# Attention scores and their masks issued in four column tiles of 32 keys instead of one of 128

## The chip, the cores and the metric

The kernel runs on one core of a Trainium2 chip. The metric is the device time of one launch in microseconds (us), as a median of several runs. The engines named here are TensorE (PE: matmuls; PEld: the weight loads that go with them), VectorE (DVE), ScalarE (ACT), GpSimd (POOL) and SyncE (SP), which issues the DMAs.

## What is computed

Two attention layers over a graph, for 8 batches of 1024 nodes with 128 features. The first has 8 heads of 16 features, the second one head with additive scores. Cut to what matters:

```python
def first(x, adj):                       # 8 heads of 16
    q, k, v = heads(x @ Wq), heads(x @ Wk), heads(x @ Wv)
    scores = einsum('bhqd,bhkd->bhqk', q, k) / sqrt(16)
    scores = where(adj[:, None] > 0, scores, -1e9)
    return merge(softmax(scores) @ v) @ Wo + bo

def second(x, adj):
    h = x @ W.T
    e = (h @ a1)[:, :, None] + (h @ a2)[:, None, :]
    e = where(e >= 0, e, 0.2 * e)
    return softmax(where(adj > 0, e, -9e15), axis=2) @ h

x = layernorm(x + first(x, adj))
x = layernorm(x + second(x, adj))
```

The change touches the product of q and k and the masking of the scores in the first layer.

## The kernel before

Each engine runs a list of instructions that is written out in full, for 8 batches with 64 positions each. Position u of batch b holds one **unit**: the scores of one head against 128 keys, for all 1024 queries. Four heads share a tile of keys, so units 4n to 4n+3 are the four heads of key tile n (n from 0 to 15: two groups of heads, eight tiles of keys).

What stands at a position on TensorE, in this order:

- `unit(b, u)`, lines 402 to 421. Two matmuls (L415, halves of 512 queries each) put the scores, keys on the partitions, into one of three PSUM slots. The stationary operand is `kst`, 97 rows by 128 keys in bf16; the moving one is `qst`, 97 rows by 512 queries. In 27 of the 64 units, those with an "m" in `MASKED_BY`, two more matmuls (L420) add the mask to the same PSUM, with the identity `same` as the stationary operand. In the other units VectorE multiplies by the mask afterwards (L755).
- `context(b, n)`, lines 423 to 443, at each position with a remainder of 3 by 4, some positions later than its units: the weights of four heads times v. It is already issued in column tiles: head i writes 17 partitions of `acc` from partition 32 i on. In the trace it is 16 matmul records (two for each fp32 matmul of the program), in four rounds of four.
- **Jobs** from the table `PE_AT`: projections q, k, v0 and v1 (L485, L499, L505), the column sums cc (L492), the transposes ctx0, ctx1, ctxT and x1T (L512, L518, L526), wo (L522), h0 and h1 (L532, and L535 with a stationary operand of one column), fi (L540), and the eight sums of the second layer, out0 to out7 (L474, L475). In a batch in the middle of the program jobs stand at the positions 1, 4 to 8, 13, 15, 17, 18, 26, 27, 28, 32, 43, 58 and 63. They are fp32 with 128 stationary columns, but for cc (bf16, 32 columns) and L535.

The language gives each matmul a tile shape by the number of its stationary columns: 128 rows by 128 columns of the array for more than 64, 128 rows by 32 columns for 32 and fewer. Below these are called **wide** and **narrow**. Units and nearly all jobs are wide; contexts, cc and L535 are narrow.

ScalarE takes each unit's slot through the exponential (L584) into `weights`, in the order of the units, with jobs of its own between them; among these are the exponentials of the second layer (exp0 to exp7, L602), at the positions 43 to 61. A slot becomes free for the unit three uses later when ScalarE is done with it (`free_for`, semaphore `exp_done`). TensorE waits for the eight exponentials of the second layer before out1 at position 63, and before the other out jobs at the positions after it.

Of the kernel before, what the change touches and what calls it, by code (L numbers as in the profile page):

```python
# [99 lines left out]
def build_fast(nc, sems, needed, x, xT, adjT, Wq, Wk, Wv, Wo, bo, W, a, out):  # L100
# [5 lines left out]
    T = N // 128  # L106
    HALF = N // 2
# [8 lines left out]
    VW = 32  # L116
# [10 lines left out]
    with ExitStack() as ctx:  # L127
        def sb(name, shape, dt):
            return ctx.enter_context(nc.sbuf_tensor(name, shape, dt))

        def sem(name):
            return sems.enter_context(nc.semaphore(name))
# [8 lines left out]
        same = sb("same", [128, 128], BF16)  # L141
# [23 lines left out]
        masks = [sb(f"mask{i}", [128, T, N], BF16) for i in range(2)]  # L165
        qst = sb("qst", [SROWS, H, N], BF16)
        kst = sb("kst", [SROWS, H, N], BF16)
# [75 lines left out]
        masks_made = sem("masks_made")  # L243
# [23 lines left out]
        def slot_of(name, me, u=0):  # L267
            return slots[slot[name, me, u]]

        def free_for(name, me, u=0):  # L270

            was = holder[name, me, u]
            if was is None:
                return exp_done, 0
            return released(*was)
# [123 lines left out]
        def _(pe):  # L399
            kw = dict(start=True, stop=True)  # L400

            def unit(b, u):
                n, i = divmod(u, HG)
                g, t = divmod(n, T)
                h = g * HG + i
                ps = slot_of("unit", b, u)
                if b == 0 and u == 0:
                    pe.wait_ge(consts_made, 2)
                if u % (UNITS // NG) == 0:
                    pe.wait_ge(stack_in[g], (b + 1) * 16 * STACK_DMAS)  # L410
                pe.wait_ge(*free_for("unit", b, u))
                by_pe = MASKED_BY[u] == "m"
                for c in range(2):
                    cols = slice(c * HALF, (c + 1) * HALF)
                    mm = pe.matmul(ps[:, cols], kst[:, h, t * 128:(t + 1) * 128], qst[:, h, cols], start=True, stop=not by_pe)  # L415
                if by_pe:
                    pe.wait_ge(masks_made, b * T + t + 1)
                    for c in range(2):
                        cols = slice(c * HALF, (c + 1) * HALF)
                        mm = pe.matmul(ps[:, cols], same[:], masks[b % 2][:, t, cols], start=False, stop=True)  # L420
                mm.then_inc(full["unit"], 1)

            def context(b, n):
# [132 lines left out]
            for b in range(-1, B + 2):  # L556
                for pos in range(UNITS):
                    if 0 <= b < B:
                        unit(b, pos)
                    if at := context_at(b, pos, B):  # L560
                        context(*at)
                    for name, me in jobs_at(PE_AT, b, pos, B):
                        job(name, me)
                        if me == 0 and name == "k":
                            fold_second_layer()
                    if b == -1 and pos == UNITS - 1:
                        pe.wait_ge(usq_made, 1)
                        pe.matmul(acc[:, 384:386], ones[:], usq[:], **kw).then_inc(unorm_mm, 1)
# [1100 lines left out]
```

## Time and profile before

| | us |
|---|---|
| median of 3 runs | 925.04 (923.72 to 925.59) |
| the profiled execution's own time | 921.75 |
| its span, first to last instruction | 920.0 |
| TensorE busy (matmuls) | 844.0, 5485 records |
| weight loads busy | 406.5, 5485 records |
| VectorE busy | 686.2 |
| ScalarE busy | 635.3 |

Matmuls are pipelined: a record lasts longer than the time to the start of the next one, and a busy TensorE is not one at its peak. So the text goes by the starts. A line of a timeline gives the start of a group of instructions and the time from there to the group's end; the difference between the starts of two lines is what the first one costs TensorE. In a line such as "128\*17 128x512 f32 x16" the first pair is rows and columns of the stationary operand, the second is the moving operand, and the last is the number of records.

### The profile page before, as it was taken

How to read it: one execution, taken by the hardware profiler on the slowest of the kernel's cores; microseconds unless marked ns; L12 is line 12 of the kernel's file. 1: busy time of each engine (PE TensorE's matmuls, PEld its weight loads, DVE VectorE, ACT ScalarE, POOL GpSimd, SP SyncE). 2: the span in 40 equal slices, each digit the busy share in tenths (PEclk: the TensorE clock that was granted, in tenths of full speed). 3: DMA queues.
4: the chain of work that ended last, by engine and by line, in shares of the span. 5: the costliest groups of instructions: out<-in, count | busy, mean ns of one | idle time of the engine just before them, and what ended most of it. 6: DMA issues, size and time to landing. Idle time of an engine off the chain costs nothing.

```text
span 920.0 us, 14889 instructions
## 1 busy us (share of the span) xinstructions
PE 844.0 (92%) x5485; PEld 406.5 (44%) x5485; DVE 686.2 (75%) x1157; ACT 635.3 (69%) x702; POOL 65.5 (7%) x47
## 2 busy tenths in 40 slices
PE   5499999999999999999999999999999999998683
PEld 2132334327533474336543374334743366324573
DVE  5276797895878868896878868787687966796463
ACT  2378886995579846896579945898378965796050
POOL 3000010001010100101010010101010010101000
PEclk9599999999999999999999999999999999999877
DMA  4877258603556227544377136363275234401000
GB/s 158 158 135 154 38 163 161 111 7 109 110 120 105 81 92 94 138 58 126 82 149 100 39 102 118 115 94 90 83 136 110 44 105 96 54 2 35 1 24 26
DMA packets 50926, 85.56 MB, mean 93 GB/s; under 512 B 5969, under 2 KB 23122, under 8 KB 50834
## 3 DMA queue, kind: packets, MB, share of 16 engines
q1 hardware_dynamic: 50850, 84.57, 44.2%
q8 instruction: 45, 0.74, 0.4%
q14 instruction: 31, 0.25, 0.1%
HBM read 67.63 MB, written 16.91 MB: 92 GB/s over the span
## 4 chain that ended last, share of the span: by engine, by line
PE 69%; ACT 16%; issue 8%; DVE 5%; DMA 0%; POOL 0%; POOLq 0%; SPq 0%; ACTq 0%; DVEq 0%
PE acc L441 18%; PE slot L415 17%; PE slot L474 11%; ACT weights L584 11%; PE slot L420 8%; ACT atts L602 4%; PE slot L485 3%; PE slot L522 2%; PE slot L532 2%; DVE weights L755 1%; PE slot L475 1%; PE slot L458 1%; PE slot L512 1%; DVE atts L769 1%; PE slot L526 1%
## 5 line engine op out<-in xcount | busy, mean ns | idle before, releaser
L584 ACT ACTIVATE weights<-slot 128x1024 f32<-128x1024 f32 x512 | 496.1, 1048 | 169.4 <-PE slot L415 94.1
L755 DVE SCALAR_TENSOR_TENSOR weights<-mask,weights 128x1024 f32<-128x1024 bf16 x296 | 359.3, 1239 | 65.4 <-ACT weights L584 64.2
L415 PE MATMUL slot<-qst,kst 97*128 97x512 bf16 x1024 | 287.3, 383 | 26.9 <-issue 14.6
L441 PE MATMUL acc<-weights,vst 128*17 128x512 f32 x2048 | 244.6, 595 | 7.1 <-DVE weights L755 6.5
L415 PEld LDWEIGHTS slot<-qst,kst 97*128 97x128 bf16 x1024 | 84.7, 98 | 213.2 <-ACT weights L584 87.2
L420 PE MATMUL slot<-mask,same 128*128 128x512 bf16 x432 | 129.8, 381 | 0.0
L474 PEld LDWEIGHTS slot<-hst,atts 128*128 128x128 f32 x896 | 105.8, 191 | 19.4 <-issue 9.2
L474 PE MATMUL slot<-hst,atts 128*128 128x129 f32 x896 | 110.7, 276 | 3.0 <-ACT atts L602 3.0
L441 PEld LDWEIGHTS acc<-weights,vst 128*17 128x17 f32 x2048 | 47.9, 96 | 141.1 <-issue 127.5
L769 DVE SCALAR_TENSOR_TENSOR atts<-turn,hst,mask 128x1024 f32<-128x1024 f32 x64 | 83.5, 1310 | 6.8 <-ACT hst L652 6.8
L845 DVE RECIPROCAL rout<-slot 128x1 f32<-128x1 f32 x62 | 10.4, 167 | 91.0 <-PE slot L475 82.4
L602 ACT ACTIVATE atts<-atts,expbias 128x1024 f32<-128x1024 f32 x64 | 75.4, 1224 | 1.7 <-DVE atts L769 1.1
L420 PEld LDWEIGHTS slot<-mask,same 128*128 128x128 bf16 x432 | 42.4, 98 | 52.1 <-issue 1.1
L708 POOL TENSOR_TENSOR rstd<-vareps,exponent 128x4 f32<-128x4 f32 (+1 forms) x24 | 33.9, 1413 | 393.6 <-DVE vareps L825 393.6
L713 POOL TENSOR_TENSOR x_sb<-x_sb,bo_all 128x1024 f32<-128x1024 f32 x8 | 22.5, 2808 | 437.9 <-DMA x_sb<-in_x 437.9
L780 DVE TENSOR_SCALAR mask<-raw 128x1024 bf16<-128x1024 int32 x64 | 48.1, 753 | 6.4 <-DMA raw<-in_adjT 6.4
L618 ACT ACTIVATE atts<-slot 128x1024 bf16<-128x1024 f32 x16 | 16.4, 1023 | 23.6 <-PE slot L485 23.6
L830 DVE TENSOR_SCALAR x<-y,meanvar,rstd 128x128 f32<-128x128 f32 x64 | 17.1, 343 | 14.5 <-POOL rstd L708 14.5
L793 DVE TENSOR_TENSOR atts<-slot,atts 128x1024 f32<-128x1024 f32 x16 | 19.6, 1224 | 11.2 <-issue 11.0
L641 ACT ACTIVATE turn<-slot 128x1024 f32<-128x1024 f32 x8 | 8.2, 1023 | 26.0 <-PE slot L518 26.0
L846 DVE SCALAR_TENSOR_TENSOR x<-slot,rout,x 128x128 f32<-128x128 f32 x62 | 21.8, 351 | 2.2
L864 DVE TENSOR_REDUCE widest<-slot 64x1 f32<-64x1024 f32 x8 | 9.7, 1216 | 17.2 <-issue 10.0
(117 smaller groups left out, 580.3 us busy)
## 6 DMA issues: line engine op xcount, KB each, us to landing
raw<-in_adjT SPq DMA_DIRECT2D x64, 512.0 KB, 4.1
parts_scratch<-atts SPq DMA_DIRECT2D x48, 256.0 KB, 2.5
qst<-parts_scratch SPq DMA_DIRECT2D x96, 128.0 KB
kst<-parts_scratch SPq DMA_DIRECT2D x96, 128.0 KB
xT_sb<-in_xT SPq DMA_DIRECT2D x8, 512.0 KB, 4.6
x_sb<-in_x SPq DMA_DIRECT2D x8, 512.0 KB, 5.4
out<-x SPq DMA_DIRECT2D x16, 256.0 KB, 2.3
qst<-shift_scratch SPq DMA_DIRECT2D x16, 8.0 KB
```

The source lines that it names most:

```text
L415: mm = pe.matmul(ps[:, cols], kst[:, h, t * 128:(t + 1) * 128], qst[:, h, cols], start=True, stop=not by_pe)
L420: mm = pe.matmul(ps[:, cols], same[:], masks[b % 2][:, t, cols], start=False, stop=True)
L441: mm = pe.matmul(acc[VW * i:VW * i + HD + 1, cols], vst[b % 2][:, t, g * HG + i], weights[:, HG * buffer(b, n) + i, cols], start=(t == 0), ...
L474: pe.matmul(to, att_of(j, k), hst[:, j, 0:D + 1], start=(j == 0), stop=False)
L485: mm = pe.matmul(ps[:, cols], (wq if name == "q" else wk)[:], xT_sb[:, cols], **kw)
L584: act.activation(to, ps[:], ACT.Exp, scale=SCALE).then_inc(exp_done, 1)
L602: act.activation(atts[:, :, j, :], atts[:, :, j, :], ACT.Exp, bias=expbias[:, j:j + 1]).then_inc(atts_made, 1)
L708: pool.tensor_tensor(rstd[i][:, tt], vareps[i][:, tt], exponent[:, tt], ALU.pow).then_inc(rstd_made[k], 1)
L713: pool.tensor_tensor(x_sb[:], x_sb[:], bo_all[:].unsqueeze(1).to_broadcast([128, T, D]), ALU.add).then_inc(xb_made, 1)
L755: dve.scalar_tensor_tensor(out=to, in0=masks[b % 2][:, n % T], scalar=0.0, in1=at, op0=ALU.is_equal, op1=ALU.mult).then_inc(masked, 1)
L769: dve.scalar_tensor_tensor(out=atts[:, :, j, :], in0=fi_all[:].rearrange("p (q n) -> p q n", q=4), scalar=hst[:, j, D + 1:D + 2], in1=mask ...
L780: dve.tensor_scalar(masks[b % 2][:, t], raw[m][:], 0, -BIG, ALU.is_le, ALU.mult).then_inc(masks_made, 1)
```

## The change

In `unit` each matmul is split into four by keys: tile i takes 32 columns of `kst` and writes the partitions 32 i to 32 i + 31 of the slot. The mask matmuls are split in the same way by columns of `same`. The order is by halves of the queries, and within one by tiles. The wait for the mask (`masks_made`) stands ahead of the scores instead of between scores and mask. Everything else, the tables included, stays.

```diff
                 pe.wait_ge(*free_for("unit", b, u))
                 by_pe = MASKED_BY[u] == "m"
+                if by_pe:
+                    pe.wait_ge(masks_made, b * T + t + 1)
                 for c in range(2):
                     cols = slice(c * HALF, (c + 1) * HALF)
-                    mm = pe.matmul(ps[:, cols], kst[:, h, t * 128:(t + 1) * 128], qst[:, h, cols], start=True, stop=not by_pe)
-                if by_pe:
-                    pe.wait_ge(masks_made, b * T + t + 1)
-                    for c in range(2):
-                        cols = slice(c * HALF, (c + 1) * HALF)
-                        mm = pe.matmul(ps[:, cols], same[:], masks[b % 2][:, t, cols], start=False, stop=True)
+                    for i in range(4):
+                        rows = slice(VW * i, VW * (i + 1))
+                        keys = slice(t * 128 + VW * i, t * 128 + VW * (i + 1))
+                        mm = pe.matmul(ps[rows, cols], kst[:, h, keys], qst[:, h, cols], start=True, stop=not by_pe)
+                for c in range(2 if by_pe else 0):
+                    cols = slice(c * HALF, (c + 1) * HALF)
+                    for i in range(4):
+                        rows = slice(VW * i, VW * (i + 1))
+                        mm = pe.matmul(ps[rows, cols], same[:, rows], masks[b % 2][:, t, cols], start=False, stop=True)
                 mm.then_inc(full["unit"], 1)
```

The program's TensorE list around the positions 15 to 17 of a middle batch, before. A row names the line, the operands (out <- in), the columns of the stationary operand by those of the moving one, and the semaphores that it waits for. L441 is the context, L518 the job ctxT, L522 the job wo.

```order
L420 MATMUL slot<-mask,same 128x512
L441 MATMUL acc<-weights,vst 17x512 [waits masked,exp_done]
L441 MATMUL acc<-weights,vst 17x512 x7
L518 MATMUL slot<-ident,turn 128x128 [waits ctx0_taken,q_taken]
L518 MATMUL slot<-ident,turn 128x128 x3
L518 MATMUL slot<-ident,turn 128x128 [waits ctx1_taken]
L518 MATMUL slot<-ident,turn 128x128 x3
L415 MATMUL slot<-qst,kst 128x512 [waits exp_done]
L415 MATMUL slot<-qst,kst 128x512
L420 MATMUL slot<-mask,same 128x512 [waits masks_made]
L420 MATMUL slot<-mask,same 128x512
```

The same place after, where the lines are five higher (L415 is L420, L420 is L425, L441 is L446, L518 is L523, L522 is L527):

```order
L425 MATMUL slot<-mask,same 32x512 x8
L446 MATMUL acc<-weights,vst 17x512 [waits masked,exp_done]
L446 MATMUL acc<-weights,vst 17x512 x7
L523 MATMUL slot<-ident,turn 128x128 [waits ctx0_taken,q_taken]
L523 MATMUL slot<-ident,turn 128x128 x3
L523 MATMUL slot<-ident,turn 128x128 [waits ctx1_taken]
L523 MATMUL slot<-ident,turn 128x128 x3
L420 MATMUL slot<-qst,kst 32x512 [waits masks_made,exp_done]
L420 MATMUL slot<-qst,kst 32x512 x7
L425 MATMUL slot<-mask,same 32x512 x8
L420 MATMUL slot<-qst,kst 32x512 [waits exp_done]
L420 MATMUL slot<-qst,kst 32x512 x7
L527 MATMUL slot<-wo,turn 128x128 [waits ctxT_taken]
```

No instruction changed places. The shape changes from wide to narrow and back have: before, one stood ahead of the context (128 to 17 columns) and one behind it; after, none stands ahead of the context, one ahead of the transposes, one behind them, and one more ahead of wo, which had none before. Over the whole program, counted in the two lists, 274 changes of shape become 224: batch by batch 29 become 9 in batch 0, 35 become 23 in batch 1, 34 become 32 in each of the batches 2 to 6, and 38 become 30 in batch 7 with what follows it; 2 stand ahead of the first unit in both.

## Rows read from the trace of the kernel before

**Rows 1.** Busy time of each engine in stretches of the span.

```profile
core 0: us, PE busy (x) PEld busy (x) DVE busy (x) ACT busy (x) POOL busy (x), PEclk, DMA share, GB/s
43.00:117.60 74.60, 72.64 (x443) 24.07 (x442) 53.44 (x55) 61.72 (x67) 0.00 (x0) 1.00 0.61 121
...
314.30:390.62 76.32, 75.84 (x509) 40.81 (x510) 57.31 (x114) 49.19 (x54) 6.93 (x4) 1.00 0.53 119
390.62:420.70 30.08, 27.95 (x177) 9.20 (x175) 27.30 (x28) 29.88 (x34) 0.00 (x0) 1.00 0.38 51
```

**Rows 2.** Timeline of TensorE near the end of the second stretch.

```profile
413.62 1.91 PE L441 MATMUL acc<-weights,vst 128*17 128x512 f32 x16 [0.72 <-DVE weights L755]
...
420.70 2.02 PE L474 MATMUL slot<-hst,atts 128*128 128x129 f32 x16 [0.55 <-ACT atts L602]
```

**Rows 3.** Timeline of ScalarE at the same place.

```profile
416.54 1.94 ACT L584 ACTIVATE weights<-slot 128x1024 f32<-128x1024 f32 x2 [0.20 <-PE slot L420]
```

**Rows 4.** Timeline of TensorE: two units, a context, the next unit.

```profile
362.65 1.03 PE L415 MATMUL slot<-qst,kst 97*128 97x512 bf16 x4
363.52 0.60 PE L420 MATMUL slot<-mask,same 128*128 128x512 bf16 x2
364.05 1.91 PE L441 MATMUL acc<-weights,vst 128*17 128x512 f32 x16
365.89 0.60 PE L415 MATMUL slot<-qst,kst 97*128 97x512 bf16 x2
```

**Rows 5.** Timeline of TensorE: context, cc, and the wait behind fi.

```profile
370.33 1.91 PE L441 MATMUL acc<-weights,vst 128*17 128x512 f32 x16
372.06 0.60 PE L492 MATMUL slot<-atts,headsum 128*32 128x512 bf16 x4
372.59 0.61 PE L415 MATMUL slot<-qst,kst 97*128 97x512 bf16 x2
...
375.40 1.51 PE L415 MATMUL slot<-qst,kst 97*128 97x512 bf16 x6 [0.48 <-ACT negshift L624]
```

**Rows 6.** Timeline of TensorE: an out job behind another, and one behind a context.

```profile
431.82 1.95 PE L474 MATMUL slot<-hst,atts 128*128 128x129 f32 x16
433.61 0.39 PE L475 MATMUL slot<-hsum,ones 128*128 128x129 f32 x2
...
440.39 2.05 PE L474 MATMUL slot<-hst,atts 128*128 128x129 f32 x16
442.28 0.39 PE L475 MATMUL slot<-hsum,ones 128*128 128x129 f32 x2
```

**Rows 7.** Timeline of TensorE: transposes behind a context and wo; transposes behind a unit.

```profile
351.37 1.09 PE L518 MATMUL slot<-ident,turn 128*128 128x128 f32 x8
352.30 0.60 PE L415 MATMUL slot<-qst,kst 97*128 97x512 bf16 x2
...
353.16 0.59 PE L415 MATMUL slot<-qst,kst 97*128 97x512 bf16 x2
353.66 2.02 PE L522 MATMUL slot<-wo,turn 128*128 128x128 f32 x16
355.52 0.60 PE L415 MATMUL slot<-qst,kst 97*128 97x512 bf16 x2
...
368.50 1.03 PE L526 MATMUL slot<-ident,x 128*128 128x128 f32 x8
369.37 0.60 PE L415 MATMUL slot<-qst,kst 97*128 97x512 bf16 x2
```

**Rows 8.** Timeline of TensorE: h0 and h1, then their one-column matmul.

```profile
379.13 1.95 PE L532 MATMUL slot<-wh,turn 128*128 128x130 f32 x16
381.01 0.38 PE L535 MATMUL slot<-wh,x1sum 128*1 128x128 f32 x2
381.32 1.04 PE L415 MATMUL slot<-qst,kst 97*128 97x512 bf16 x4
```

**Rows 9.** Groups by line: the context's matmuls.

```profile
L441 PE MATMUL acc<-weights,vst 128*17 128x512 f32 x2048 | 244.6, 595 | 7.1 <-DVE weights L755 6.5 <-ACT weights L584 0.6
```

## The prediction

> **What bounds the kernel now.** I read the busy time by stretch first, then the timeline of TensorE inside each stretch, by the starts of its groups. A batch in the middle of the program lasts 106.40 us and has two parts. In the first, 76.32 us from the job out1 to the exponential of unit 40, TensorE is busy for 75.84 us and ScalarE for 49.19; in the second, 30.08 us, ScalarE is busy for 29.88 and TensorE for 27.95 [rows 1]. So TensorE sets the first part. In the second, where the exponentials of the second layer stand, ScalarE does, and TensorE waits for others: 0.72 us ahead of a context and 0.55 us ahead of out1 [rows 2]. Work taken off TensorE pays in the first part alone. Batch 0 has no second part: TensorE is busy for 72.64 of 74.60 us, ScalarE for 61.72 [rows 1].
>
> **What a unit costs.** Two pairs of wide matmuls take 363.52 − 362.65 = 0.87 us, so 0.435 a pair [rows 4]. For a pair in narrow tiles the nearest row is the context: with nothing to switch behind it, its four rounds of four tiles take 372.06 − 370.33 = 1.73 us [rows 5], 0.4325 a round. A round of fp32 there lasts as long as two of bf16, and four tiles run in it at once. The last of the four starts about 1.91 − 3 × 0.4325 − 0.595 = 0.02 us behind the first [rows 4, 9], and this lag is not paid again in each round, or the four would not fit in 1.73. So a narrow pair should cost 0.432: 0.003 less than a wide one. Bounds: no gain, and a loss of 0.04 (the lag paid in both rounds; third rival). The first part of a batch has 41 units and 20 masks, 61 pairs: −0.18 us; batch 0, with all its 91 pairs, −0.27.
>
> **What a change of shape costs.** Into a context: 364.05 − 363.52 is 0.53, 0.095 over the pair. Out of a context to a unit: 365.89 − 364.05 is 1.84, 0.11 over 1.73 [rows 4, 5]. From a wide job to a narrow matmul: 381.01 − 379.13 is 1.88 behind h1, against 433.61 − 431.82 = 1.79 for as many records without a switch, 0.09 [rows 6, 8]. Into an fp32 job more is lost than the 0.11: the out job behind a context takes 442.28 − 440.39 = 1.89 against 1.79, 0.10 more [rows 6], and eight transposes take 352.30 − 351.37 = 0.93 against 369.37 − 368.50 = 0.87, 0.06 more [rows 7]. I read these as the first weights, which cannot be loaded while the array still drains. So a context among wide units costs 0.095 + 0.11 = 0.205. After the change, a wide job among narrow units costs 0.11 + 0.10 + 0.095 = 0.305, or 0.265 where it begins with transposes. The job's price is the context's turned round, plus the load.
>
> The Trainium skill says in "TensorEngine Tiling (Array Packing)", section Tiling Modes, that changing the mode, not just the tile, drains TensorE; it has no figure, and says nothing of a load behind the drain. By that rule alone jobs would cost what contexts did, which is the first rival; the 0.10 of the out job speaks against it.
>
> **The sum for a middle batch (2 to 6), first part.** Removed: ten contexts, at the positions 3 to 39. Ten entries, 10 × 0.095 = 0.95; seven exits to units, 0.77; exits to out6 (position 7) 0.21 and to ctxT (15) 0.17. The exit at 27 leads to cc, which is narrow already, and costs nothing. Also gone: the exit of L535 behind h1 (0.10, bounded by cc's exit, 372.59 − 372.06 less 0.43 [rows 5]). Its entry, 0.09, stays and is counted on both sides. Together 2.29. Added: six jobs that begin with matmuls (positions 1, 4, 5, 7, 13, 18), 1.83; three with transposes (6, 8, 26), 0.795; ctxT 0.265; h0 and h1, 0.21 + 0.09 = 0.30; the exit of out1 into unit 0, 0.095. For wo, of 0.305, some 0.14 is paid today: it waits 353.66 − 353.16 − 0.435 = 0.065 and takes 355.52 − 353.66 = 1.86 against 1.79 [rows 7]; 0.165 is left. Job fi adds nothing: TensorE waits 0.48 us behind it for ScalarE's negshift [rows 5], whose chain begins at cc, and both switches, 0.31, fit into that wait with cc's exit, 0.10, that goes. If this cover were gone, 0.31 us a batch. Together 3.45. Net +1.16, less 0.18 for the pairs.
>
> Second part: ScalarE's row is broken once, for 0.20 us, by a unit that TensorE brings late [rows 3], just behind the context at 413.62. That context's exit goes: −0.11. The other switches of this part lie under ScalarE's work. So a middle batch gains 1.16 − 0.18 − 0.11 = **+0.87 us**, five of them +4.35.
>
> **The other batches.** Batch 0 has 15 contexts and few jobs. Gone: 15 entries 1.425, 13 exits 1.43, one exit to v0 0.21; together 3.065 (the 16th exit-like switch, cc's, lies in the wait for negshift). Added: q, k and v1, 0.915, and v0, 0.305. Net −1.845, with the pairs −2.1. Batch 1 has no out jobs within its first part: removed 2.19 (no 0.10 of load for out6), added ctx0 and ctx1 0.53, q 0.305, ctxT and wo 0.43, k 0.305, x1T 0.265, h 0.30, so 2.135; with −0.18 and −0.11, −0.35. Batch 7 is a middle one without k (−0.305), with fi uncovered (+0.305, no cc) and the exit at 27 gone as well (−0.11): +0.76.
>
> **Total:** 4.35 − 2.1 − 0.35 + 0.76 = +2.7 us. The profiled execution took 921.75 us, 3.3 below the median of the runs shown; the sum is made against it, 924.4, and carried to the median: 925.04 + 2.7 = **927.7 us**.
>
> **What costs nothing.** The mask's wait now stands ahead of the scores. Behind it on TensorE's queue stand the whole unit and all that follows; but TensorE never waited at the mask's matmuls inside a unit (they start 0.435 behind the scores [rows 4]), so the mask is ready before. What could make it late is VectorE, whose masks precede their units by several positions. Each pair has four times the instructions; in the context 16 matmuls and 16 loads pass in 1.73 us, 54 ns each, and a narrow pair needs 16 in 0.432, 27 ns each. No row shows that rate held for long; it is part of the third rival. ScalarE gets each unit at most 0.02 us later, which matters only where it waits on TensorE.
>
> **The rivals.**
>
> First, not slower: entering a job behind a bf16 unit costs no load. The 0.10 was seen behind the context's fp32 rounds alone. Then each middle batch loses 0.97 of the 3.45 and 0.16 of the 2.29, and comes out at +0.06 (five: +0.3), batch 0 at −2.4, batch 1 at −0.85, batch 7 at −0.05: −3.0 in all, **922.0 us**. It decides once an entry costs under about 0.05. Against it: both kinds of fp32 job show the loss. Further down still, if all 50 switches fewer were bare gains of 0.1, −5 and −1.6 for the pairs, 918.5.
>
> Second, neutral: the terms are as I have them but batch 0 and the covers give 1 to 2 us more than I counted, 926. It is the lower half of my forecast, not a mechanism of its own.
>
> Third, much slower: the four tiles' lag of 0.02 us is paid in every round, because a round of bf16 lasts half as long as the context's, or instructions cannot follow at 27 ns. With 91 + 7 × 61 = 518 pairs on the path, 0.04 each is +20.7: **948 us**. At the context's 54 ns an instruction a pair would take 0.86 and the kernel some 220 us more. Against it: cc's four bf16 matmuls, in two tiles, pass in 0.53 with an exit in it, so two rounds take 0.43 [rows 5]; but that is two tiles, not four. The Trainium skill reports in "TensorE: Matmul & The Clock Gate", section Measured speedup vs the span model, a speedup of 2.38 for three column tiles, not 3. An estimate by that page would make a round about a quarter longer and the kernel some 57 us slower; the context's rounds show no such loss.
>
> Fourth, that the tiles do not run side by side at all: excluded by the context, where four tiles take 1.73 us and not four times that.
>
> **How the numbers follow.** Forecast 0.62, with its own range of 925 to 931 (the pairs' gain nil, +1.6; fi's cover gone, +1.9; loads smaller, −2). First rival 0.14, second 0.06, third with its smaller forms 0.18. The range for 8 in 10 is 921 to 940: it takes in half of the first rival, and the third up to some 0.025 us a pair. A measurement of this kernel can tell about 0.2%, 1.85 us: 923.2 and 926.9 are the bounds. Of the forecast a bit over half lies above 926.9, nearly all the rest between; with the rivals: faster 0.13, same 0.34, slower 0.53.
>
> **What would show it.** On TensorE's timeline after: pairs at 0.43; unit to context without the 0.095; context to unit in 1.73; an out job behind a unit in 1.89 instead of 1.79, its exit 0.09 more; h1 to the next unit without a switch. By stretch: a first part of about 77.3 us, a second of 30.0, a middle batch of 107.3, batch 0 two us shorter. Wrong if pairs are above 0.44 (third rival), if entries to jobs cost under 0.16 (first), or if TensorE's waits in the first part grow.

## The result and the profile after

The changed kernel takes **931.03 us** (median of 4 runs, 928.91 to 931.21) against 925.32 us for the kernel before on the same chip (median of 4, 923.72 to 925.95): a ratio of 1.0059, with a 95% interval of 1.004 to 1.0079. It is slower by 5.7 us, where 2.7 was forecast. The profiled executions took 928.91 and 921.75 us, 7.2 apart.

The head of the page of the changed kernel; TensorE has 9853 matmuls and as many weight loads instead of 5485:

```profile
span 927.2 us, 23841 instructions
...
PE 847.1 (91%) x9853; PEld 437.9 (47%) x9853; DVE 687.1 (74%) x1157; ACT 638.1 (69%) x702; POOL 64.9 (7%) x47
```

The stretches that answer to [rows 1], with the same columns: batch 0 from the exponential of unit 4 on, then the two parts of a middle batch.

```profile
43.08:117.50 74.42, 70.66 (x960) 27.99 (x955) 53.18 (x55) 62.25 (x68) 0.00 (x0) 1.00 0.60 121
316.06:393.35 77.29, 76.89 (x882) 43.30 (x882) 58.12 (x114) 49.54 (x55) 6.97 (x4) 1.00 0.50 118
393.35:423.32 29.97, 27.74 (x357) 10.35 (x349) 27.30 (x28) 29.87 (x35) 0.00 (x0) 1.00 0.38 54
```

The first part is 0.97 us longer than before (77.29 against 76.32), the second 0.11 shorter (29.97 against 30.08); both are what was forecast. Batch 0 is not: it was to lose two microseconds. In this table the length of a batch is the time from its first exponential to that of the next batch, in the two profiled executions (the first and the last two rows say where they begin and end; exponentials are taken at their starts):

| stretch | before | after | change | forecast |
|---|---|---|---|---|
| up to the first exponential | 37.75 | 37.96 | +0.21 | 0 |
| batch 0 | 79.87 | 79.54 | −0.33 | −2.1 |
| batch 1 | 93.01 | 94.16 | +1.15 | −0.35 |
| batches 2 to 5, each | 106.39 | 107.25 | +0.86 | +0.87 |
| batch 6 | 106.39 | 107.88 | +1.49 | +0.87 |
| batch 7, to its last exponential | 98.59 | 99.20 | +0.61 | +0.76 |
| from there to the end | 78.86 | 79.45 | +0.59 | 0 |

The prices of the switches come out as forecast. TensorE's timeline after, units, a context, the next unit, as [rows 4]:

```profile
366.00 1.05 PE L420 MATMUL slot<-qst,kst 97*32 97x512 bf16 x16
366.87 0.61 PE L425 MATMUL slot<-mask,same 128*32 128x512 bf16 x8
367.31 1.89 PE L446 MATMUL acc<-weights,vst 128*17 128x512 f32 x16
369.02 0.61 PE L420 MATMUL slot<-qst,kst 97*32 97x512 bf16 x8
```

Two narrow pairs take 0.87 us, as two wide ones did. The context follows a pair after 0.44 us instead of 0.53, and the next unit follows the context after 1.71 instead of 1.84. The same timeline at an out job behind units, which answers to [rows 6], and at wo and x1T, which answer to [rows 7]:

```profile
345.91 1.04 PE L420 MATMUL slot<-qst,kst 97*32 97x512 bf16 x16
346.87 2.05 PE L479 MATMUL slot<-hst,atts 128*128 128x129 f32 x16
348.76 0.39 PE L480 MATMUL slot<-hsum,ones 128*128 128x129 f32 x2
...
356.26 0.60 PE L420 MATMUL slot<-qst,kst 97*32 97x512 bf16 x8
356.80 2.05 PE L527 MATMUL slot<-wo,turn 128*128 128x128 f32 x16
358.78 0.61 PE L420 MATMUL slot<-qst,kst 97*32 97x512 bf16 x8
...
371.19 0.61 PE L425 MATMUL slot<-mask,same 128*32 128x512 bf16 x8
371.73 1.09 PE L531 MATMUL slot<-ident,x 128*128 128x128 f32 x8
372.75 0.61 PE L420 MATMUL slot<-qst,kst 97*32 97x512 bf16 x8
```

The out job takes 348.76 − 346.87 = 1.89 behind a unit, as behind a context before. Job wo starts 0.54 behind its unit's pair and takes 1.98, 0.19 more than a job without switches: 0.105 + 0.19 = 0.295 in all, forecast 0.305. The transposes x1T take 1.02, 0.15 more than among wide units: 0.255 with the entry, forecast 0.265.

**Where the rest went.** In batch 0 and in batch 1 TensorE stops in the middle of a group. Its timeline, first in a unit's mask matmuls, then in a context:

```profile
70.02 0.61 PE L420 MATMUL slot<-qst,kst 97*32 97x512 bf16 x8
70.45 0.38 PE L425 MATMUL slot<-mask,same 128*32 128x512 bf16 x2
72.52 0.61 PE L425 MATMUL slot<-mask,same 128*32 128x512 bf16 x6 [1.68 <-issue]
```

```profile
151.96 0.59 PE L446 MATMUL acc<-weights,vst 128*17 128x512 f32 x1
153.05 1.48 PE L446 MATMUL acc<-weights,vst 128*17 128x512 f32 x12 [0.49 <-issue]
```

From the start of the second tile of a mask's round to that of the third pass 2.06 us, and from the first tile of a context's first round to the second 1.08; in the other masks and contexts of the eight batches it is 0.02 or less, but for 0.19 in the mask that follows the first pause. "issue" means that the profile shows nothing that TensorE waited for; a semaphore cannot be it, since no wait stands inside a group. The two together are 3.1 us of the 4.5 by which the forecast missed the 7.2 of the profiled executions. Both stand at the same remainder: counting TensorE's recorded instructions (matmuls, weight loads, waits) from the first, the pauses come ahead of number 961 and number 3009, 193 + 3 × 256 and 193 + 11 × 256.

The queues of the page, before and then after, with their packets, MB and share, show what has this period:

```profile
q8 instruction: 45, 0.74, 0.4%
```

```profile
q8 instruction: 80, 1.31, 0.6%
```

Queue 8 brings 16 KB a packet (1.31 MB by 80), one for some 256 instructions of TensorE: its program has 11789 instructions before and 20741 after. So a packet is used up in about 920.0 / 45 = 20 us before and 927.2 / 80 = 11.6 after. Read over the eight batches of the changed kernel, the packet of a block starts at about the time at which the block ahead of it begins: for 52 of 74 blocks between 2.4 us before that and 1.6 us after. The others start later, up to 8.4 us after, and the blocks of the two pauses are among the latest three. For the block whose first instruction is number 961 the block ahead begins at 61.8, and this is what the DMA engines did from then to 69.3 us, and from 69.3 to 71.2:

```profile
DMA packets 530, 0.86 MB, mean 114 GB/s; under 512 B 111, under 2 KB 111, under 8 KB 530
## 3 DMA queue, kind: packets, MB, share of 16 engines
q1 hardware_dynamic: 530, 0.86, 103.9%
```

```profile
q1 hardware_dynamic: 22, 0.04, 9.8%
q8 instruction: 1, 0.02, 5.6%
```

All sixteen engines were busy, with packets under 8 KB, and no packet of instructions is among them. What SyncE had issued last before this is thirteen loads of `qst` and `kst`, the first and the last of them:

```profile
54.69 0.38 SPq L345 DMA_DIRECT2D qst<-parts_scratch  x1
60.78 0.28 SPq L347 DMA_DIRECT2D qst<-shift_scratch  x1
```

The packet of instructions starts at 69.4, when the burst is over, lasts 1.7 us, and TensorE goes on 1.4 us after that. In batch 1 the same happens with the block behind the one that begins at 141.5: its packet starts at 149.9. Before the change the shortest block of the batches lasts 15.6 us, and no packet landed less than 9.6 us ahead of its block.

The Trainium skill says in "Advanced Engine Details and Errata", section ISA Cache, that a line of the instruction cache is 16 KB, which is 256 instructions, and that there are only two lines. The packets (80 of 16 KB for 20741 instructions) and the period of the pauses agree with the first; no run here shows the number of lines.

Batch 6 is 0.62 us longer than its neighbours because of something else: VectorE waits there for a late transfer of `in_adjT`, once. It did not come again when the kernel ran again (below).

### The profile page after: what moved, and what is told of

Its sections match the earlier page's. It is cut to its first block, busy times and chain, and to the rows that moved or that the text cites. A ratio compares the mean times of both kernels' runs of the same rounds, so it can differ in the third digit from the quotient of the medians.

```text
span 927.2 us, 23841 instructions
## 1 busy us (share of the span) xinstructions
PE 847.1 (91%) x9853; PEld 437.9 (47%) x9853; DVE 687.1 (74%) x1157; ACT 638.1 (69%) x702; POOL 64.9 (7%) x47
## 3 DMA queue, kind: packets, MB, share of 16 engines
q8 instruction: 80, 1.31, 0.6%
## 4 chain that ended last, share of the span: by engine, by line
PE 65%; ACT 17%; issue 11%; DVE 5%; DMA 0%; POOL 0%; ACTq 0%; POOLq 0%; SPq 0%; DVEq 0%
PE slot L420 16%; PE acc L446 15%; PE slot L479 12%; ACT weights L589 11%; PE slot L425 7%; ACT atts L607 4%; PE slot L490 3%; PE slot L527 2%; PE slot L537 2%; PE slot L517 2%; PE slot L480 1%; PE slot L463 1%; DVE weights L760 1%; PE slot L531 1%; DVE atts L774 1%
## 5 line engine op out<-in xcount | busy, mean ns | idle before, releaser
L420 PE MATMUL slot<-qst,kst 97*32 97x512 bf16 x4096 | 303.9, 383 | 29.2 <-issue 14.5
L446 PE MATMUL acc<-weights,vst 128*17 128x512 f32 x2048 | 245.3, 592 | 6.9 <-DVE weights L760 5.7
L420 PEld LDWEIGHTS slot<-qst,kst 97*32 97x32 bf16 x4096 | 102.4, 96 | 197.7 <-issue 71.0
L425 PE MATMUL slot<-mask,same 128*32 128x512 bf16 x1728 | 139.0, 381 | 1.7 <-issue 1.7
L479 PEld LDWEIGHTS slot<-hst,atts 128*128 128x128 f32 x896 | 104.3, 191 | 25.0 <-issue 13.9
L479 PE MATMUL slot<-hst,atts 128*128 128x129 f32 x896 | 112.9, 279 | 2.7 <-ACT atts L607 2.7
L446 PEld LDWEIGHTS acc<-weights,vst 128*17 128x17 f32 x2048 | 58.5, 97 | 118.0 <-issue 89.9
L425 PEld LDWEIGHTS slot<-mask,same 128*32 128x32 bf16 x1728 | 50.5, 97 | 49.0 <-issue 3.2
```

The source lines that it names most:

```text
L420: mm = pe.matmul(ps[rows, cols], kst[:, h, keys], qst[:, h, cols], start=True, stop=not by_pe)
L425: mm = pe.matmul(ps[rows, cols], same[:, rows], masks[b % 2][:, t, cols], start=False, stop=True)
L446: mm = pe.matmul(acc[VW * i:VW * i + HD + 1, cols], vst[b % 2][:, t, g * HG + i], weights[:, HG * buffer(b, n) + i, cols], start=(t == 0), ...
L479: pe.matmul(to, att_of(j, k), hst[:, j, 0:D + 1], start=(j == 0), stop=False)
```

## The experiments

Two theories stand against each other for what the profile shows. By the **switch theory** each change of the tiles' shape has the prediction's price, and everything else is pauses in the **stream of instructions**. By the rival, narrow tiles, or their many instructions, cost something of their own in every pair. Each kernel is compared with the kernel before on its own chip.

**Units in two column tiles of 64.** A shape that neither contexts nor jobs have.

```diff
-                    for i in range(4):
-                        rows = slice(VW * i, VW * (i + 1))
-                        keys = slice(t * 128 + VW * i, t * 128 + VW * (i + 1))
+                    for i in range(2):
+                        rows = slice(64 * i, 64 * (i + 1))
+                        keys = slice(t * 128 + 64 * i, t * 128 + 64 * (i + 1))
...
```

(The mask's matmuls are split in the same way.)

> Scores and masks in two column tiles of 64 keys; the jobs stay at 128, the contexts at 32, so units have a shape that neither neighbour has. Switch theory (every change of the tiles' shape costs what the prediction priced, 0.095 to 0.11 us, and 0.10 more where an fp32 job's first weights follow): the contexts keep their entry and exit, 0.205 each, and the jobs pay 0.265 to 0.305 as in the changed kernel, so a middle batch is about 3.45 - 0.18 = 3.3 us longer than before (109.7), batch 0 about 1 us longer, the whole about 945 to 948 us. Rival (only the step between the undivided and a divided array costs, 64 to 32 does not): the time of the changed kernel without its two stalls, 927 to 931 us, context entries at 0.435. Rival (what costs is the number of instructions, not the switches): half of the changed kernel's added instructions, 926 to 929 us.

Measured: 945.5 us, 1.0227 (1.0195 to 1.0259). A middle batch lasts 109.67 us, 3.28 more than before; batch 0 80.22, batch 1 94.70. Its timeline at a context:

```profile
372.69 0.60 PE L425 MATMUL slot<-mask,same 128*64 128x512 bf16 x4
373.22 1.91 PE L446 MATMUL acc<-weights,vst 128*17 128x512 f32 x16
375.06 0.62 PE L420 MATMUL slot<-qst,kst 97*64 97x512 bf16 x4
```

0.53 into the context and 1.84 for it, exactly as in [rows 4], while the jobs pay as after. So it is the change of shape that costs, from 64 to 32 columns as from 128 to 32, and not the step from an undivided array to a divided one. The Trainium skill says in "TensorEngine Tiling (Array Packing)", section Tiling Modes, that a change of the tiling mode drains TensorE; the price seen here, 0.095 us into and 0.11 us out of the context, agrees with it.

**Undivided units with as many instructions.** Score and mask in pieces of 128 queries.

```diff
-                for c in range(2):
-                    cols = slice(c * HALF, (c + 1) * HALF)
-                    mm = pe.matmul(ps[:, cols], kst[:, h, t * 128:(t + 1) * 128], qst[:, h, cols], start=True, stop=not by_pe)
...
+                for c in range(8):
+                    cols = slice(c * 128, (c + 1) * 128)
+                    mm = pe.matmul(ps[:, cols], kst[:, h, t * 128:(t + 1) * 128], qst[:, h, cols], start=True, stop=not by_pe)
+                    if by_pe:
                         mm = pe.matmul(ps[:, cols], same[:], masks[b % 2][:, t, cols], start=False, stop=True)
```

(The mask's wait stands ahead of the unit, as in the changed kernel.)

> Units undivided (128 keys) as in the kernel before, but each score and each mask in eight matmuls of 128 queries instead of two of 512: the same number of TensorE instructions as the changed kernel (20741), and not one switch moved; the mask's wait stands ahead of the unit as in the changed kernel. Switch theory: middle batch as before, 106.4 us plus at most 61 pairs times 0.015 (0.9). Instruction theory (the stream of instructions comes in blocks of 256, and a block that is fetched behind a burst of transfers comes late): one or more pauses of 0.5 to 3 us in the middle of a group with no semaphore behind them, all at the same remainder of the instruction count by 256, in batches 0 and 1; 926 to 934 us in all. Rival (narrow tiles themselves cause the pauses): none here, batch 0 at 79.9 us and batch 1 at 93.0.

Measured: 940.75 us, 1.0175 (1.0135 to 1.0216), more than either theory gave. A middle batch is 108.27, 1.88 over before. Its timeline in batch 0:

```profile
73.16 0.22 PE L417 MATMUL slot<-qst,kst 97*128 97x128 bf16 x1
73.22 0.22 PE L419 MATMUL slot<-mask,same 128*128 128x128 bf16 x1
73.69 0.22 PE L417 MATMUL slot<-qst,kst 97*128 97x128 bf16 x1 [0.25 <-issue]
```

Where scores and masks alternate, a piece takes 0.058 us instead of 0.054 (an eighth of 0.435), so a masked unit 0.93 instead of 0.87: 1.2 us for the 20 in a first part, and some 0.3 for pieces of 0.056 in the others. The remaining 0.4 were not located. The four narrow tiles do not pay this, so the kernel is a poor stand-in for them in time. But it answers its question: without one narrow tile more it stops for 0.47 us, again ahead of instruction 961. That is one short pause, where one or more of 0.5 to 3 us were expected in the batches 0 and 1, but it shows that a pause does not need the narrow tiles.

**Narrow only between narrow neighbours.** A unit is in four tiles of 32 only where what TensorE does ahead of the unit and behind it is narrow too (`narrow` lists these units).

```diff
+                width = VW if (b, u) in narrow else 128
...
-                    for i in range(4):
-                        rows = slice(VW * i, VW * (i + 1))
-                        keys = slice(t * 128 + VW * i, t * 128 + VW * (i + 1))
+                    for i in range(128 // width):
+                        rows = slice(width * i, width * (i + 1))
+                        keys = slice(t * 128 + width * i, t * 128 + width * (i + 1))
...
```

> Units in four tiles of 32 keys only where what stands ahead of them and behind them on TensorE (context, cc, the exit of h1) is in such tiles as well; all other units undivided as before. 150 switches instead of 274 (before) and 224 (changed). Switch theory: no job pays anything new; a middle batch gains 0.7 us against before (contexts at 19, 23, and from h1's exit to 39), batch 0 about 2 us, batches 1 and 7 about 0.7 each, in all about 6 us: 918 to 920 us. If blocks of instructions come late (16145 instructions, between 11789 and 20741), batch 0 keeps fewer or none of the two stalls of 2.06 and 1.08 us. Rival (narrow pairs have a cost of their own): no gain, 924 to 928 us.

Measured: **919.48 us**, 0.9942 (0.992 to 0.9963): faster than both kernels. A middle batch lasts 105.54, 0.85 less than before, where 0.7 was expected, batch 1 92.47. The narrow pairs have no cost of their own. Batch 0 however takes 80.08. It stops for 1.79 us, ahead of instruction 705 = 193 + 2 × 256:

```profile
72.39 0.38 PE L449 MATMUL slot<-mask,same 128*32 128x512 bf16 x2
74.18 0.61 PE L449 MATMUL slot<-mask,same 128*32 128x512 bf16 x6 [1.41 <-issue]
...
79.41 1.52 PE L444 MATMUL slot<-qst,kst 97*32 97x512 bf16 x16 [1.82 <-ACT negshift L653]
80.70 1.93 PE L470 MATMUL acc<-weights,vst 128*17 128x512 f32 x8
```

Behind the second wait the granted clock is down: eight records of the context last 1.93, as long as sixteen do elsewhere. The start of this stretch, with the columns of [rows 1]:

```profile
79.40:81.20 1.80, 1.79 (x20) 0.74 (x24) 1.01 (x2) 1.80 (x3) 0.00 (x0) 0.62 0.16 55
```

The 0.62 is a mean over both of the clock's levels: from 79.9 to 83.2 the granted clock is 0.50, the lower one (1.2 of 2.4 GHz), and 1.00 around it. With a mean of 0.63 from 81.2 to 84.0, an estimate of the loss is 0.38 × 1.8 + 0.37 × 2.8 = 1.7 us.

**Two job groups fewer.** The changed kernel with out4 and out6 next to other jobs.

```diff
-    1: [("out0", -2)], 4: [("out3", -2), ("out7", -2)], 5: [("out4", -2)], 6: [("ctx0", -1)], 7: [("out6", -2)],
-    8: [("ctx1", -1), ("out5", -2)], 13: [("out2", -2), ("q", 1)], 15: [("ctxT", -1)], 17: [("wo", -1)],
+    1: [("out0", -2)], 4: [("out3", -2), ("out7", -2), ("out4", -2)], 6: [("ctx0", -1)],
+    8: [("out6", -2), ("ctx1", -1), ("out5", -2)], 13: [("out2", -2), ("q", 1)], 15: [("ctxT", -1)], 17: [("wo", -1)],
```

> The changed kernel with the job out4 moved from position 5 to 4, behind out3 and out7, and out6 from 7 to 8, ahead of ctx1: two wide groups fewer among the narrow units of each batch with out jobs, 24 switches fewer, the same work. Switch theory: 2 x 0.305 = 0.61 us less in each of the batches 2 to 7, so 3.7 us less than the changed kernel: about 927 us, middle batch 106.65. Rival (the price is by job and not by group, or other waits take its place, since the exponentials then wait for a longer group): no change, 931 us, middle batch 107.25.

Measured: 926.51 us, 1.0024 (1.0007 to 1.0042), and a middle batch of 106.68: 0.57 less than after, of 0.61 expected. The price is by group. Three out jobs in a row (positions 4 and 5 before) now have one entry and one exit:

```profile
325.10 2.05 PE L479 MATMUL slot<-hst,atts 128*128 128x129 f32 x16
...
327.21 1.95 PE L479 MATMUL slot<-hst,atts 128*128 128x129 f32 x16
329.00 0.39 PE L480 MATMUL slot<-hsum,ones 128*128 128x129 f32 x2
329.22 1.95 PE L479 MATMUL slot<-hst,atts 128*128 128x129 f32 x16
```

The second takes 329.00 − 327.21 = 1.79, without a load ahead of it. The pauses stand ahead of the instructions 961 and 3009 again, with 1.47 us and 1.36 from start to start, and a third of 1.00 stands ahead of 16577 in batch 6.

**The stream shifted by half a block.**

```diff
-                    pe.wait_ge(consts_made, 2)
+                    for i in range(128):
+                        pe.wait_ge(consts_made, 2)
+                        pe.wait_ge(consts_in, 64)
```

(One wait of each pair rides on the instruction behind it, so 128 instructions are added.)

> The changed kernel with 128 waits that are already satisfied ahead of the first unit, where TensorE waits for its data anyway: no work is changed, but every later instruction stands 128 further in TensorE's stream, half a block of 256. Instruction theory: the pauses without a semaphore leave the matmuls at which they stood (the masks of 70.74, the context of 152.25) and stand again at a recorded count of 193 modulo 256, so about 128 instructions earlier or later in the work; their lengths change, because a block that is needed at 67 instead of 72.8 us is needed while the burst of transfers still holds it: 0 to 5 us each, the whole 927 to 937 us. Rival (the pause belongs to its place in the work, a semaphore that the profile does not show): pauses of 2.0 and 1.1 us at the same matmuls, 931 us.

Measured: 931.46 us, 1.0091 (1.0059 to 1.0124). The pauses are gone from where they stood: batch 0 takes 76.67 us and batch 1 93.07. They stand elsewhere, ahead of the instructions 6593, 13249 and 18369 (0.94, 1.08 and 2.49 us from start to start), all of them 193 and a multiple of 256. The longest is in batch 7, where the block ahead begins at 787.2:

```profile
795.87 0.38 PE L422 MATMUL slot<-qst,kst 97*32 97x512 bf16 x2
798.36 0.61 PE L422 MATMUL slot<-qst,kst 97*32 97x512 bf16 x6 [2.12 <-issue]
```

The DMA queues from 787.3 to 795.0 us, and from 795.0 to 797.2:

```profile
q1 hardware_dynamic: 561, 0.92, 106.4%
```

```profile
q1 hardware_dynamic: 34, 0.05, 14.0%
q8 instruction: 1, 0.02, 5.2%
```

No work was changed and no transfer was moved in the program, so the place of a pause is set by the position in the stream of instructions, and not by a semaphore that the profile misses. Which borders of blocks meet a burst was not foreseen: the pauses over 0.9 us sum to 4.5 us here and to 3.1 in the changed kernel.

**The mixed kernel with an undivided start.** Units 0 to 31 of batch 0 stay wide.

```diff
-                width = VW if (b, u) in narrow else 128
+                width = VW if (b, u) in narrow and (b or u >= 32) else 128
```

> The mixed kernel (narrow units only between narrow neighbours), with the units 0 to 31 of batch 0 undivided as before: eight switches more, and 288 instructions fewer ahead of the burst of transfers of batch 0. Instruction theory: the pause of 1.57 us that the mixed kernel has in batch 0, and the half clock behind the two long waits there, go; batch 0 takes 79.87 - 1.3 = 78.6 us instead of 80.08, the other batches stay at 92.5 and 105.54: 1.5 us less than the mixed kernel, about 918 us, 0.993 of before. Rival (the mixed kernel's batch 0 lost its gain to something else, such as ScalarE, and not to the pause): batch 0 at 80 or more, 919.5 to 921 us.

Measured: **917.74 us**, 0.9941 (0.9921 to 0.9961). Batch 0 takes 77.59 us, 2.5 less than in the mixed kernel: no pause stands in it, and the clock does not fall behind the wait for negshift. (The expected 78.6 was worked out against a batch 0 whose first units still ran at the lower clock: units 0 to 4 take 4.39 us here and 5.12 in the kernel before.) A new pause of 1.39 us stands in batch 5, ahead of instruction 9665 = 193 + 37 × 256, between the two mask matmuls of an undivided unit:

```profile
575.36 0.38 PE L449 MATMUL slot<-mask,same 128*128 128x512 bf16 x1
576.75 0.39 PE L449 MATMUL slot<-mask,same 128*128 128x512 bf16 x1 [1.01 <-issue]
```

The ratios of the two mixed kernels cannot be told apart; both beat the kernel before by about 0.6% and the changed one by more than 1%.

**The mask's wait alone.** The kernel before, with this wait ahead of the scores.

```diff
                 by_pe = MASKED_BY[u] == "m"
+                if by_pe:
+                    pe.wait_ge(masks_made, b * T + t + 1)
...
-                    pe.wait_ge(masks_made, b * T + t + 1)
```

> The kernel before, with one part of the change alone: the wait for the mask stands ahead of a unit's scores. The prediction put it at nothing: middle batch 106.39, batch 0 79.87, 924 us. Rival (VectorE makes the masks just in time, or the 216 waits that now are instructions of their own cost issue time): up to 0.05 us for each of some 20 masked units in a first part, a middle batch of 106.4 to 107.4, 924 to 931 us.

Measured: 925.66 us, 1.001 (0.9994 to 1.0025); a middle batch lasts 106.39. The moved wait costs nothing that shows.

**The changed kernel again**, with no edit.

> The changed kernel once more. Instruction theory: the pauses at the recorded counts 961 and 3009 come again, 2.0 and 1.1 us within 0.4, since the stream and the transfers are the same; the 0.62 us of batch 6 (a wait of VectorE for a late transfer of in_adjT) need not. 929 to 931 us.

Measured: 930.47 us, one run. The pauses ahead of 961 and 3009 are there, with 1.78 and 1.43 us from start to start, and a third of 0.92 ahead of 16577 in batch 6, which then takes 107.41; the late transfer is not. Middle batches take 107.25.

## Why the prediction was right, and where it was not

The median of 931.03 us lies inside the range of 921 to 940, and at the upper edge of the forecast's own 925 to 931. The switches are what was forecast; the rest of the way to this edge has a cause that the forecast did not have.

- **What bounds the kernel**: right. The first part took the 0.97 us and the second gave 0.11.
- **A pair costs the same, narrow or wide**: right (0.87 for two). The mixed kernels, where narrow pairs come with switches removed and none added, gain what the switches are worth, so the third rival's lag in every round is out.
- **The prices of a change of shape**, and the first fp32 load behind it: right to about 0.01 us for out, wo and x1T. The first rival (no load behind the drain) would have given a middle batch of +0.06; it was +0.86. The load itself shows in the trace of the kernel before: behind the context the first load of the out job's weights starts with its first matmul, at 440.39; behind the other out job it starts 0.11 ahead, at 431.71 for 431.82. After the change it starts with the matmul behind a unit too, at 346.87. That fi's switches hide in the wait for negshift holds: from the start of cc to the unit behind that wait it takes 3.34 us before (372.06 to 375.40) and 3.33 after (375.35 to 378.68).
- **The mask's wait is free**: right, by the run with the wait alone.
- **Batch 1**: forecast −0.35, and +0.06 where no pause disturbs it (the shifted kernel, 93.07). Of the 0.41, 0.2 is the context at position 3: its first four units take 4.63 us in both kernels, about what four units take in a second part (4.65), where ScalarE sets the pace, so TensorE's gain is not seen. Another 0.11 is the exit in its second part: the units 56 to 60 take 6.31 us in both. The rest, 0.1, was not located.
- **Batch 0**: forecast −2.1, measured −0.33, with a pause of 2.06 in it. The kernel with the wait alone (79.00, wide) and the shifted kernel (76.67, narrow, no pause) start nearly alike (units 0 to 4 take 4.39 and 4.27 us; before and after the change, both 5.12), and differ by −2.33: the gain is there, and the pause took it.
- **The step that failed** is the one that put the fourfold instructions at nothing, but for the third rival's price in every pair. The engine does follow at 27 ns an instruction, pair after pair. What does not follow is the supply of blocks, at a few places: where a burst of transfers meets the border of a block. The term was 0 in the sum; it measured 3.1 us in the profiled execution, 2.06 in batch 0 and 1.08 in batch 1. Without it 7.2 would be 4.1, of which 0.6 is the late transfer and 0.8 lies ahead of the first unit and behind the last: 2.7 are left, the forecast. That it is met so closely is in part luck: batch 1 missed by +0.4, and the batches 0 and 7 by −0.3 and −0.15. The two ends of the span vary without reference to the change: over ten profiles, of before, after and the experiments, the time up to the first exponential was 37.7 to 40.3 us, and that behind the last 76.8 to 81.2. That is why the lengths of the batches are a sharper measure here than the medians.

That the loads of `qst` and `kst` hold the packet of instructions back is read from the traces: at each of the 13 pauses over 0.9 us the packet started 6.5 to 12 us after the block ahead had begun, the sixteen DMA engines were full until then, and the packet started as the burst ended. The kernel before, the tiles of 64 and the run with the wait alone have no pause of this kind; their blocks last 13.9 us or more in the batches, and no packet landed less than 6.3 us ahead of its block. The transfers themselves were not taken away or moved, so this part was not tried.

## What to carry to other kernels

Tiling a matmul more finely for the sake of one neighbour's shape moves the change of shape to its other neighbours; count the changes of shape along the engine's whole list, give each its price from the trace (here 0.2 us for a context, 0.3 for an fp32 job), and change the shape only where both neighbours already have it. Then count the instructions as well as the columns: where their number nearly doubles, look at how long a block of the instruction stream lasts beside the longest burst of transfers. Pauses that the profile puts down to issue, inside a group, and that return at the same remainder of the instruction count, were the sign of it here.

## What the runs showed of the hardware

- TensorE's instructions came in packets of 16 KB for 256. In the pauses over 0.9 us TensorE went on 1.2 to 1.5 us after the packet had landed; the packet itself took 1.1 to 1.9 us, and had waited for the end of a burst of small packets on all sixteen DMA engines.
- Behind two gaps close together TensorE's clock was lower in some kernels and not in others. In the mixed kernel a pause of 1.79 us and then a wait of 1.82 for negshift, which ends five microseconds later, were followed by a granted clock of 0.50, the lower of its two levels (1.2 of 2.4 GHz), from 79.9 to 83.2 us; in the kernel with two job groups fewer pause and wait were 1.47 and 1.82, and the clock was 0.50 from 78.0 to 81.3. In the changed kernel, with 2.06 and 1.82 at the same place, and when it ran again, with 1.78 and 1.81, it stayed at 1.00. What decides it was not settled.
- A bf16 matmul of 128 columns whose weights change with each one took 0.058 us instead of the 0.054 that its share of a longer one is.
